# A hybrid block on one Trainium2 core: loads in pieces, attention products finished block by block, ten warm-up calls, new orders

## The reference

```python
attn = einsum('ds,td->st', w1, w2) * sparse_mask        # 512 x 512, computed once
x = x + gelu(layernorm(x) @ attn + b2)                  # stage 1
x = x + clustered_dense(layernorm(x), weight, bias, centroids, assignments)   # stage 2
x = x + single-head attention(layernorm(x), Wqkv, bqkv, Wo, bo)               # stage 3, per batch
x = x + clustered_dense(layernorm(x), ...)                                    # stage 4, same weights
```

## Time and profile before

| | before |
|---|---|
| median of 3 runs | 283.52 us (281.71 to 283.75) |
| the profiled execution, time | 282.99 us |
| its span in the trace | 281.2 us |
| mean granted TensorE clock | 0.988 |
| TensorE busy | 268.5 us (95%) |
| VectorE, ScalarE, GpSimd busy | 228.3, 147.7, 159.3 us |

### The profile page before, as it was taken

One profiled execution on the slowest core, in us unless ns is written; L12 is line 12 of the kernel. 1 busy time (PEld: TensorE's weight loads), 2 busy tenths in 40 slices (PEclk: granted clock), 3 DMA queues, 4 the chain that ended last, 5 costly groups with the idle time before them and its releaser, 6 DMA issues.

```text
span 281.2 us, 4344 instructions
## 1 busy us (share of the span) xinstructions
PE 268.5 (95%) x1380; PEld 224.5 (80%) x1380; DVE 228.3 (81%) x454; ACT 147.7 (53%) x272; POOL 159.3 (57%) x192
## 2 busy tenths in 40 slices
PE   5978999999999989999989999999999999999992
PEld 5867888788888878788978888888888888888781
DVE  1966899976779997677879989989767797897896
ACT  3582676343367747347566962882464626155400
POOL 2282989098836654189997997781072015506620
PEclk9997999999999999999999999999999999999997
DMA  7999700740000000000000000000000000000078
GB/s 214 395 332 331 240 1 1 286 164 1 0 2 0 1 2 0 0 2 0 1 0 3 0 2 0 0 3 0 0 5 0 0 2 0 0 0 2 2 287 310
DMA packets 10118, 18.23 MB, mean 65 GB/s; under 512 B 1072, under 2 KB 1840, under 8 KB 10096
## 3 DMA queue, kind: packets, MB, share of 16 engines
q1 hardware_dynamic: 10096, 17.96, 17.9%
HBM read 13.76 MB, written 4.19 MB: 64 GB/s over the span
## 4 chain that ended last, share of the span: by engine, by line
PE 72%; DVE 10%; POOL 10%; issue 6%; ACT 1%; POOLq 1%; DVEq 0%; ACTq 0%
PE m_bank L932 54%; PE t_bank L1025 9%; PE m_bank L1105 5%; POOL y_tok L513 3%; POOL y_tok L526 3%; DVE x_tok L916 2%; PE m_bank L985 2%; POOL rstd L440 2%; DVE odd_lo L749 2%; POOL ve L439 1%; PE t_bank L1031 1%; DVE st L742 1%; PE m_bank L924 1%; POOL nbias L443 1%; DVE qsel L864 1%
## 5 line engine op out<-in xcount | busy, mean ns | idle before, releaser
L742 DVE BATCH_NORM_STATS2 st<-x_tok 128x6 f32<-128x512 f32 x64 | 43.7, 682 | 0.2
L526 POOL TENSOR_TENSOR y_tok<-y_tok,x_tok 128x512 f32<-128x512 f32 x16 | 20.4, 1297 | 32.6 <-ACT y_tok L691 32.6
L932 PE MATMUL m_bank<-ffn_hi,even_hi 128*128 128x512 f32 x96 | 38.7, 403 | 0.0
L932 PE MATMUL m_bank<-ffn_lo,even_hi 128*128 128x512 f32 x96 | 37.6, 392 | 0.0
L932 PE MATMUL m_bank<-ffn_hi,even_lo 128*128 128x512 f32 x96 | 37.5, 390 | 0.0
L506 POOL TENSOR_TENSOR y_tok<-y_tok,bias_f 128x512 f32<-128x512 f32 x16 | 21.0, 1321 | 14.4 <-ACT y_tok L636 14.4
L439 POOL TENSOR_SCALAR ve<-mv 128x1 f32<-128x1 f32 (+1 forms) x31 | 10.1, 326 | 33.7 <-DVE mv L743 32.4
L440 POOL TENSOR_TENSOR rstd<-ve,half 128x1 f32<-128x1 f32 (+1 forms) x31 | 23.1, 746 | 2.6
L585 ACT ACTIVATE even_hi<-t_bank 128x512 fp32r<-128x512 f32 x24 | 13.6, 595 | 16.7 <-PE t_bank L1025 15.1
L553 ACT ACTIVATE xn_odd<-x_tok,nbias,rstd 128x512 f32<-128x512 f32 x20 | 16.2, 817 | 10.8 <-POOL nbias L443 10.7
L932 PE MATMUL m_bank<-odd_hi,wqkv_hi 128*128 128x512 f32 (+1 forms) x60 | 21.5, 359 | 0.0
(11 more groups left out here) (172 smaller groups left out, 754.9 us busy)
## 6 DMA issues: line engine op xcount, KB each, us to landing
out<-x_tok SPq DMA_DIRECT2D x15, 256.0 KB, 2.5
x_tok<-in_L_attn_a_x SPq DMA_DIRECT2D x3, 1024.0 KB, 10.3
xn_odd<-in_L_attn_a_xt SPq DMA_DIRECT2D x2, 1024.0 KB, 8.1
w_raw<-in_L_attn_a_w SPq DMA_DIRECT2D x4, 256.0 KB, 4.7
y_tok<-in_L_attn_a_w SPq DMA_DIRECT2D x4, 256.0 KB, 4.8
x_tok<-in_L_attn_a_x SPq DMA_DIRECT2D x2, 512.0 KB, 6.7
y_tok<-in_L_attn_a_sparse_mask SPq DMA_DIRECT2D x1, 1024.0 KB, 9.2
xt_other<-in_L_ffn_weight SPq DMA_DIRECT2D x1, 1024.0 KB, 11.3
```

The costliest lines, as they stand in the source:

```text
L526: pool.tensor_tensor(y_tok[:, n, :], y_tok[:, n, :], x_tok[:, n, :], ALU.add).then_inc(done[kind], 1)
L742: link(dve.bn_stats(st[:, at % 2, :], x_tok[:, n, :]))
L932: ins = pe.matmul(bank, a, w, start=(first and n == 0), stop=(last and n == count - 1))
```

## The change

- The four-piece loads: the mask, the dense weight and the first tokens come as four DMAs of 256 KB each (before: one, one and two). The first token tile is the first load of all. `mask_attn.i` waits for its own piece, and `fsum` for the pieces it reads.
- `last.i` now holds the last two chunks (six products) of row block i; step `attn.2` is gone. `rawhi.i` no longer waits for all `last`: `raw_hi/raw_lo` 0 and 1 overwrite w1's chunks 0 and 1, and 2 and 3 go to space of the later weights. The sums `a_sum`, `f_sum` move likewise, and `latehi`/`latelo`, which fill that space, get one more wait, for the y1 steps of batch 0. Banks 0 to 3 are tied to `last.0..3`.
- Warm-up: ten calls, both operands `mean_raw`, after GpSimd's first memset alone, which now is that of `mean_raw`; the wait for all constants stands behind them. `nbias` shares the storage of `ve`.
- All five orders are new.

```diff
-WARM = 4
+WARM = 10
-attn.0.0 attn.0.1 attn.0.2 attn.1 attn.2 last.0 T.x1.0.1 last.1 T.x1.0.0 last.2 last.3 T.x1.0.2 T.x1.0.3
-y1.0.2.c2 y1.0.0.c2 y1.0.2.c3 colmean y1.0.0.c30 y1.0.2.c0 y1.0.1.c3 y1.0.3.c1 y1.0.0.c1 y1.0.2.c1 y1.0.1.c02
+attn.0.0 T.x1.0.0 attn.0.1 attn.0.2 attn.1 T.x1.0.3 T.x1.0.1 last.0 last.1 last.2 last.3 y1.0.3.c0 T.x1.0.2
+y1.0.3.c1 y1.0.0.c01 y1.0.1.c1 y1.0.0.c2 y1.0.3.c3 y1.0.0.c3 y1.0.3.c2 y1.0.1.c0 T.cen.0.0 y1.0.1.c2 colmean
+y1.0.2.c2 ffnmean y1.0.1.c3 y1.0.2.c3 T.x2.0.3 y1.0.2.c10 y1.1.0.c2 y1.1.3.c20 y1.1.0.c10 y1.1.1.c1 y1.1.3.c1
...
-bestT.4 dn4.3.0.c3 mask.4 dn4.3.0.c1 dn4.3.1.c3 dn4.3.0.c2 dn4.3.1.c01 dn4.3.2.c31 dn4.3.0.c0 dn4.3.2.c2
-dn4h.3.3.0 dn4h.3.3.1 dn4.3.2.c0
+... bestT.4 dn4.3.0.c0 mask.4
+dn4.2.0.c02 dn4.3.1.c1 dn4.2.0.c3 dn4.3.2.c02 dn4.3.1.c32 dn4.2.0.c1 dn4h.3.3.0 dn4h.3.3.1
...
 ACT_ORDER
-w2hi.0 w1hi.0 w1hi.1 w2hi.1 w2hi.2 w1hi.2 w2hi.3 w1hi.3 norm.1.0.1 norm.1.0.0 norm.1.0.2 hi.x1.0.1 hi.x1.0.0
+w1hi.0 w2hi.0 w2hi.1 norm.1.0.0 w1hi.1 w2hi.2 norm.1.0.3 w2hi.3 w1hi.3 w1hi.2 norm.1.0.1 hi.x1.0.3 hi.x1.0.1
+rawhi.0 norm.1.0.2 hi.x1.0.0 rawhi.1 rawhi.2 hi.x1.0.2 rawhi.3 ccen fshi shi xhi.1.0 xhi.1.3 gelu.0.3 ahi.0
...
 DVE_ORDER
-w2lo.0 w1lo.0 w1lo.1 w2lo.1 w2lo.2 w1lo.2 w2lo.3 w1lo.3 stats.1.0.1 stats.1.0.0 stats.1.0.2 stats.1.0.3
+stats.1.0.0 w1lo.0 w2lo.0 w2lo.1 stats.1.0.3 stats.1.0.1 w1lo.1 w2lo.2 w2lo.3 w1lo.3 w1lo.2 stats.1.0.2 cstat
+mask_attn.0 lo.x1.0.3 mask_attn.1 rawlo.0 lo.x1.0.1 mask_attn.2 rawlo.1 lo.x1.0.0 mask_attn.3 rawlo.2 rawlo.3
+stats.1.1.2 stats.1.1.0 lo.x1.0.2 fslo scaled.0.3 slo scaled.0.0 center.0 center.2 x1.0.3 center.1 scaled.0.1
...
 POOL_ORDER
-rstd.1.0.1 rstd.1.0.0 rstd.1.0.2 rstd.1.0.3 asum.1 asum.2 asum.3 alo.2 fsum.1 fsum.2 xlo.1.0 fsum.3 alo.0
+rstd.1.0.0 rstd.1.0.3 rstd.1.0.1 fsum.1 rstd.1.0.2 fsum.2 asum.1 asum.2 cmean fsum.3 asum.3 xlo.1.0 xlo.1.3
+alo.2 alo.0 alo.1 xlo.1.1 alo.3 xlo.1.2 rstd.1.1 flo.3 flo.1 flo.0 flo.2 rstd.2.0 xlo.2.3 latehi.2 xlo.2.1
...
 SP_ORDER
-load.w2.0 load.w1.0 load.w2.1 load.w1.1 load.w2.2 load.w1.2 load.w2.3 load.w1.3 load.x0.0 load.x0.1 load.sparse
-load.ffn load.b2 load.x.1 load.xt.1 load.cen load.x.2 load.x.3 load.small load.bias load.xt.2 load.late
-load.xt.3 store.1.1 store.0.0 ...
+load.x0.0 load.w1.0 load.w2.0 load.w2.1 load.x0.3 load.x0.1 load.w1.1 load.w2.2 load.w2.3 load.w1.3 load.w1.2
+load.ffn.1 load.ffn.0 load.x0.2 load.cen load.sparse.0 load.ffn.2 load.sparse.1 load.sparse.3 load.sparse.2
+load.b2 load.x.1 load.ffn.3 load.xt.1 load.small load.x.3 load.bias load.x.2 load.late load.xt.3 load.xt.2
+store.2.1 store.0.1 ...
...
+        raw_hi = [even_hi[:, 0, :], even_hi[:, 1, :], spare_hi[:, 0:D], spare_hi[:, D:2 * D]]
+        raw_lo = [even_lo[:, 0, :], even_lo[:, 1, :], spare_lo[:, 0:D], spare_lo[:, D:2 * D]]
...
                 elif kind == "rawhi":
                     act.wait_ge(*done_at("mask_attn", (t,)))
-                    act.wait_ge(*done_at("last"))
...
-            pe.wait_ge(consts, 7)
-            for _ in range(WARM):
-                pe.matmul(m_bank[M_BANKS - 1][:, 0:P], ident[:, :], mean_raw[:, :], start=True, stop=True)
+            pe.wait_ge(pchain, 1)
+            for _ in range(WARM):
+                pe.matmul(m_bank[M_BANKS - 1][:, 0:P], mean_raw[:, :], mean_raw[:, :], start=True, stop=True)
+            pe.wait_ge(consts, 7)
...
                 elif kind == "last":
-                    c = KC - 1
+                    late = (KC - 2, KC - 1)
...
```

More of the change, by code:

```diff
@@ L58 @@
+dn4.2.1.c31 dn4.3.0.c1 dn4.3.2.c1 dn4.2.1.c0 dn4.3.1.c0 dn4.3.0.c3 dn4.3.2.c3 bestT.4 dn4.3.0.c0 mask.4
+dn4.2.0.c02 dn4.3.1.c1 dn4.2.0.c3 dn4.3.2.c02 dn4.3.1.c32 dn4.2.0.c1 dn4h.3.3.0 dn4h.3.3.1
 """
 ACT_ORDER = """
-w2hi.0 w1hi.0 w1hi.1 w2hi.1 w2hi.2 w1hi.2 w2hi.3 w1hi.3 norm.1.0.1 norm.1.0.0 norm.1.0.2 hi.x1.0.1 hi.x1.0.0
-norm.1.0.3 rawhi.1 rawhi.2 hi.x1.0.2 rawhi.3 hi.x1.0.3 shi rawhi.0 ahi.2 xhi.1.0 ahi.0 gelu.0.0 gelu.0.2 ahi.1
-xhi.1.2 fshi xhi.1.1 ahi.3 xhi.1.3 hi.x2.0.2 gelu.0.1 gelu.0.3 fhi.0 fhi.1 hi.x2.0.0 fhi.3 gelu.1.0 ccen fhi.2
@@ L64 @@
[L64 to L68, removed]
@@ L79 @@
+hi.p.3.0 qb.1.1 qb.1.2 hi.p.3.2 hi.x4.2.1 hi.x4.2.0 hi.x4.2.2 hi.x4.2.3 ohi.3 lgev.4.2 hi.x4.3.3 cexp.4.2
+hi.x4.3.0 hi.x4.3.2 qb.2.2 qb.2.1 hi.x4.3.1 qb.2.3 lgev.4.3 cexp.4.3 qb.2.0 qb.3.0 qb.3.2 qb.3.1 qb.3.3
 """
 DVE_ORDER = """
-w2lo.0 w1lo.0 w1lo.1 w2lo.1 w2lo.2 w1lo.2 w2lo.3 w1lo.3 stats.1.0.1 stats.1.0.0 stats.1.0.2 stats.1.0.3
-mask_attn.0 mask_attn.1 mask_attn.2 mask_attn.3 lo.x1.0.1 lo.x1.0.0 rawlo.2 lo.x1.0.2 rawlo.3 slo rawlo.0
-center.2 rawlo.1 lo.x1.0.3 center.0 cstat center.1 scaled.0.0 stats.1.1.1 center.3 scaled.0.2 x1.0.0 x1.0.2
@@ L111 @@
 """
 POOL_ORDER = """
-rstd.1.0.1 rstd.1.0.0 rstd.1.0.2 rstd.1.0.3 asum.1 asum.2 asum.3 alo.2 fsum.1 fsum.2 xlo.1.0 fsum.3 alo.0
-xlo.1.1 alo.1 xlo.1.2 alo.3 rstd.1.1 cmean xlo.1.3 flo.1 flo.0 flo.3 flo.2 xlo.2.2 rstd.2.0 xlo.2.0 xlo.2.3
-xlo.2.1 rstd.2.1 latehi.1 latehi.3 latehi.0 rstd.1.2 bias2.0.1 bias2.0.2 bias2.0.0 xlo.3.2 rstd.1.3 xlo.3.3
-latelo.3 xlo.3.1 latelo.1 latehi.4 latelo.4 latehi.2 bias2.0.3 bias2.1.2 xlo.3.0 latelo.2 bias2.1.1 bias2.1.3
-rstd.2.2 bias2.1.0 latelo.0 rstd.2.3 bias2.2.0 bias2.3.3 bias2.2.2 rstd.3.0.2 rstd.3.0.3 masked.1.3 rstd.3.0.1
@@ L159, in products_order @@
 def products_order():
-    taken, first, last, bank = {}, set(), set(), {}
+    taken, first, last = {}, set(), set()
+    bank = {("last", (i,)): i for i in range(TPB)}
     for at, (kind, key) in enumerate(PE_STEPS):
@@ L493, in _ @@
                         pool.wait_ge(*landed("late"))
+                        pool.wait_ge(*done_at("y1", *[(0, t) for t in every]))
                         pool.wait_ge(*done_at("ffnmean", ()))
```

191 lines of the change are left out of this document (98 added, 93 removed).

## The result

The kernel after takes 287.10 us (median of four, 285.39 to 287.44) against 283.28 (281.71 to 283.75): ratio 1.0132, 95% interval 1.0075 to 1.0190. It is slower, and the time lies outside the range. The profiled execution, the fastest of the four, took 285.39 us with a span of 283.3 and a mean granted clock of 0.991, against 282.99, 281.2 and 0.988. The other three had clocks of 0.984 to 0.986 and 1.5 to 2.1 us more; they left no trace, so where their clock fell stays open.

A forecast was written before the change was run, and what follows sets the result against it. The prediction took PE to bound the kernel, with gains only from its waits, low clock, late start and tail. Its terms summed as 282.99 - 3.5 - 0.8 + 0.7 = 279.4 us, range 277.7 to 282.6.

The forecast's parts named there:

- First term: First stage, attention matrix: y1 follows `last.3` without the 2.35 us wait or the low clock behind it; 3.5 us gained.
- the 45 that was named as a sign of being wrong: GpSimd's early chain: flo was forecast to end near 44.7; ending after 45 would show the prediction wrong.
- Second term: Middle of the kernel: one old PE wait goes, the other pays for new waits; 0.8 us gained.
- The 0.77: PE's 0.77 us wait before 99.88 in the kernel before, for x1.3.0; forecast to go in the new order.
- the 1.14: PE's 1.14 us wait before 143.70 in the kernel before, behind GpSimd's `masked` and `rstd`; left to pay for new waits.
- TensorE waits from 80 to 250 that sum to more than 2: Middle of the kernel: PE waits summing to over 2 us there were named as a sign of being wrong.
- Third term: The tail: the column mask comes three products later in PE's work and the end moves with it; 0.7 us lost.
- New waits in the middle: Rival: new PE waits in the middle equal the two old ones and more; 280.2 to 282.2 us, chance 0.17.
- The clock did not start low: Rival, first stage: PE idles after the warm-up and chunk 0 runs at low clock; 281.0 to 281.6 us, chance 0.18.
- The wait did not move to colmean: Rival, first stage: PE reaches colmean before `slo` and the 2.35 us wait returns there; 281.5 us, chance 0.05.
- flo at 45.98 came before 47: Rival, slower: GpSimd's chain to flo ends after some 47 and PE waits; 284.6 to 285.4 us, chance 0.06.
- The pieces landed: Rival, loads: the pieces load slowly and PE waits for the last mask piece; about 289 us, chance 0.01.

The follow-up runs named there:

- e4_both: The changed kernel with the edits of e2 and e3 together: 280.86 us, ratio to the kernel before 0.9944.
- e7: e4_both with each `rawhi` again waiting for all four `last`, as in the kernel before: 284.25 us, ratio to before 1.0051.
- e8: e4_both with another tail: `bestT.4` and `mask.4` six products earlier, `csel.4` and two `out` ahead of blends: 281.81 us, ratio to before 0.9970.
- e3: The changed kernel with GpSimd's bias additions moved out of the stretch of stage 2's last softmax: 283.10 us, ratio to before 1.0007.
- e13: e4_both timed once more, unchanged: 281.04 us, ratio to before 0.9944.
- e5: The kernel before with three spare 128x512 additions on GpSimd after bias2.2.0: 284.27 us, ratio to before 1.0035.
- e11: e4_both with the load of the dense weight's piece 3 moved ahead of b2 and x.1: 280.86 us, ratio to before 0.9943.
- e2: The changed kernel with hi.x3.1.3 moved behind norm.3.1.0 on ScalarE and qkdve.q.0 ahead of lo.x3.1.3 on VectorE: 283.81 us, ratio to before 1.0032.

## Why the prediction was wrong

**First term (3.5 us gained): right.** Point by point: w2.0's split was there for 6.69 (predicted 6.8), attn.1 at 10.43 (10.5), `last.3` ended near 20.0 (19.6), y1 without a wait, colmean at 28.62 (27.9). The lead at 25.8 is 2.97 us; the missing 0.5 is the later end of `last.3`: the two blocks of transposes before it took 1.24 us (13.26 to 14.50), not 1.0, and its 36 products (20.06 - 10.43 - 1.24) / 36 = 0.233, not 0.226. The balance of e4_both reads 3.89 at the same place. flo ended at 45.98 (44.7), past the 45 that was named as a sign of being wrong, and PE did not wait for it. e7 shows that most of the term is the hand-over: 2.4 us less lead, and 3.0 us more time than e4_both, with the old wait in `rawhi`.

**Second term ("The middle", 0.8 us gained): this is the step that failed.** The 0.77 went as I said, and brought 1.0. What failed is the sentence "250 us of new order hold new waits that no row shows: bound below by nothing, above by the 1.9 that the old order had". The old order's waits are no bound on those of a new one. Measured: 2.32 at 116.13, 1.84 + 0.49 at 141, and half the speed over 3.45 us, of which PE was busy 2.96, another 1.48. That is 6.1 us, less the 1.14 of the earlier trace rows that is gone. By the balance the lead goes from 2.94 at 96.5 to -0.84 at 149.4: 3.8 us lost where 0.8 were to be gained. Two of the signs spoke: TensorE waits from 80 to 250 that sum to more than 2 (4.65), and the mask, 1.9 us later than 265.46 and not 3 to 3.5 earlier. Both could have been read before the run, from the orders and the trace: the chain to `bestT.2` had 0.8 us of slack, and GpSimd's new order put five additions beside it where before had one; and hi.x3.1.3, which waits for a PE step, had been moved ahead of the norm that PE wants next. That such an addition stretches a short step stands in before's own trace, at an earlier batch, where PE did not have to wait for it:

```profile
88.92 1.30 POOL L506 TENSOR_TENSOR y_tok<-y_tok,bias_f 128x512 f32<-128x512 f32 x1 [1.02 <-ACT y_tok L636]
89.03 1.21 DVE L855 SCALAR_TENSOR_TENSOR ncmx<-cmx,rstd 128x4 f32<-128x4 f32 x1
```

I had weighed margins of tenths only in the first stage, where the change announced itself.

**Third term (0.7 us lost): right in kind, too small.** From 260.7 to the end of the span after loses 1.2 us (from -0.89 to -2.1), and e4_both the same (from 4.09 to 2.9). The three products by which the mask comes later are 0.7 of it. Another 0.36 is the wait before the mask, 0.56 where before had 0.20: `csel` takes 0.80 in the place of 0.44, again until a GpSimd addition beside it is done. `csel` in after, and in before:

```profile
266.49 0.80 DVE L887 TENSOR_SCALAR csel<-csel 64x128 fp32r<-64x128 f32 x1
...
264.92 0.44 DVE L884 TENSOR_SCALAR csel<-csel 64x128 fp32r<-64x128 f32 x1
```

From the mask to the end it is 15.9 us where it was 15.7, so "the end moves with the mask" nearly held; e8 shows that it holds only as long as the blends keep their places.

**Rivals.** "New waits in the middle" was the right one, with 280.2 to 282.2 some 5 us too low, by the same false bound. The clock did not start low in after; in the trace of e3, whose first product came at 7.12, it fell behind it (0.66 from 7 to 12), and the lead at 25.8 was 1.84 there. The wait did not move to colmean, though 0.5 us of it stood there in e4_both, where `slo` took 1.57 in the place of 0.68, beside GpSimd's `xlo`. flo at 45.98 came before 47. The pieces landed 0.68 us apart (sparse.1, .3, .2). What the Trainium skill, page "DMA: Bandwidth & Descriptors", section "Bandwidth", says on batching to at least 1 MiB showed no price here: 256 KB in 0.68 us in after, 1 MB in 2.8 in before.

**The sum** is near once both faults are mended: the profiled e4_both took 280.12 and e13 280.16 where 279.4 was predicted, with a lead at 260.7 near 4.2 (3.5 + 0.8 = 4.3 forecast) and 1.2 lost behind it. Its middle is then what the second term said, 0.77 gone (worth 1.0) and the 1.14 paid out again as 0.70 + 0.35. But e4_both's ratio stands 0.56% below before where 1.4% was forecast; part of that is the choice of the profiled 282.99 as the base, as before also runs near 281.6.

## What to carry to other kernels

When all orders are new, list the chains that PE waits for with little slack (here the softmax to the mask) and hold each against what the other engines do in that stretch in the new order: how long a step takes depends on what runs beside it. Look in each engine's order for steps that wait for PE and stand ahead of steps that PE waits for. And the waits of an old order say nothing of how large those of a new one can be.

## What the runs showed of the hardware

- An addition of 128x512 on GpSimd, 1.3 us, holds up VectorE's short steps until it is done: 0.16 to 0.93, 0.17 to 1.27, 0.42 to 1.37 us in after, 0.16 to 0.95 and 0.17 to 0.61 in e5, 0.16 to 1.21 in before at 89.03; the reductions beside such additions kept their 0.42 and 0.60. The Trainium skill, page "SBUF — State Buffer", section "Who interferes with whom", says that a VectorE instruction with two inputs in SBUF, or a copy or tensor_scalar in its two-port mode, and a GpSimd instruction that reads SBUF exclude each other, the second waiting for the end of the first, and that reductions are not touched. The traces agree in each of these cases, as far as who waits and until when; in which mode VectorE ran a step they do not show. The prediction did not use it, and it is the rule that spoke against this change.
- The low level of the clock follows on some waits and not on others: 1.84 + 0.49 us at 141 was followed by 0.51 in after, the same two waits (1.84 + 0.65) in e3 were not, nor the 2.32 at 116. Why is open.
- The first loads land at different times from one execution to the next: the load of w2.0 landed at 4.88 to 6.37 us, and attn.0.0 started at 5.63, 5.67, 5.82, 6.20, 6.59, 6.69, 6.92 and 7.12, in the traces of e4, e11, e13, e2, e7, after, e8 and e3, which have the same first loads and warm-up. attn.1 moved less, from 9.93 to 10.56, but for e3 (12.11, at the low clock). A gain in the first stage is read against that.
